# A new issue order for all engines of a post-LN attention and gated-MLP block, with the later weight loads behind the first sixteen spreads

## The chip, the cores and the metric
One NeuronCore of a Trainium2 chip runs the whole kernel in one launch. The metric is device time in microseconds (us). The kernel before takes 326.44 us, the median of 3 runs (326.33 to 326.91).

## The reference
x has shape (4, 512, 128), float32: four batches of 512 tokens. There are 16 heads of width 8.

```
qkv  = x @ qkv_w.T + qkv_b            # per head: q, k, v of width 8
attn = softmax(q @ k.T * 8**-0.5) @ v
x1   = layernorm(x + (attn @ fc_w.T + fc_b + x))
h    = silu(x1 @ w1.T * s1) * (x1 @ w2.T * s2)      # 128 -> 512
h    = gelu(h @ h1.T * t1)                          # 512 -> 512, exact gelu
h    = gelu(h @ h2.T * t2)                          # 512 -> 512
out  = layernorm(x1 + h @ w3.T * s3)                # 512 -> 128
```

## The kernel before
The work is cut into six units: batches 0 and 3 are two units of 256 tokens each, batches 1 and 2 one unit of 512 each. Every engine runs one list of named steps. The lists are text constants at the head of the file (`SP_ORDER`, `PE_ORDER`, `ACT_ORDER`, `DVE_ORDER`, `POOL_ORDER`, lines 8 to 52). `walk` reads them. A token `S:5` in the list of PE is step S with its result in PSUM bank 5, `H*3` is three further pieces of step H in the bank they already have, `zk*2` is two steps. The n-th time a name occurs, it is the n-th step of that kind (counted from 0, as S33 in the prediction). What a step computes and what it waits for is fixed by its name and number, whatever its place in the list. Engines take their list strictly in order, so the place decides what is queued behind a wait.

The steps that matter here:

- `x` transposes the 512 tokens of a batch (L443), `q` projects to q and to k (L532; two steps a batch), `v` to v (L537).
- q and k are split into bf16 parts on ACT, DVE and POOL: `q` and `da` (L728, L745), `r`, `mid`, `lo`, `db` (L857, L862, L866, L885), from batch 1 on also POOL's `da`, `mid`, `db`. The parts lie in `parts`. SP's DMAs spread them over the partitions of `stack` (L366, 128 KB each, two for each pair of heads). For batch 0 these are 16 single steps, `zq` and `zk`, eight for q and eight for k; a pair of heads needs its `zq` and its `zk`. The first `zq` waits for q's `lo` and copies, the first `zk` for k's. For batches 1 to 3 a step `spread` issues four DMAs for four heads, once the T steps of the batch before no longer read that part of `stack`.
- `S` (L479) is a tile of scores, 128 queries by 512 keys. DVE's step `s` (L852) takes its negated row maximum. When a group of heads is done, POOL's `m` splits the maxima, PE's `m` transposes them, ACT's `m` copies them and SP's `mrow` (L412) writes them into `stack` as one more row. There are 18 such groups, and the first needs 4 S tiles.
- `T` (L490) is the same scores transposed with the maximum already subtracted; its group waits for its `mrow`. ACT's `e` (L716) takes the exponential. `P` (L508) multiplies with v, `o`, `a`, `f` finish attention, and DVE's `l1` steps with POOL's `p1` make the layer norm x1. `X` transposes x1, `A` and `B` are the first two linear layers, `H` the two inner ones, `W` and `Y` the last (L468 for A, B, H and W), and `l2` with `p2` the second layer norm.
- `wt` transposes a 128 by 512 slab of weights (L443): number 0 and 1 are w1 and w2, 2 to 5 the four slabs of h1, 6 to 9 those of h2, 10 is w3. ACT copies it (L796), POOL splits it with `wc` and `wl` (L1017, L1020), and ACT's `wm` (L792) sums the magnitudes of the low part. After all eleven, DVE's `wx`, PE's `L` and DVE's `L` make a flag; PE reads it before the first `A`.
- SP loads with `lw` (w1, w2), `lh` (first h1, then h2, 1 MB each), `l3` (w3, into `y`), `more` (fc_b and the five scale vectors, six DMAs), `vb`, `xin` (the next batch's x), `xres` (the residual) and stores with `out`. `xres` n waits for x1 of the batch before it; `out` n waits for the n-th finished unit of the second layer norm. All of them, the spreads and the rows of maxima go through SP's one queue in the order of `SP_ORDER`.

Of the kernel before, what the change touches and what calls it, by code (L numbers as in the profile page):

```python
# [18 lines left out]
T:5 T:0 T:6 S:4 S:1 P T:2 S:3 T:5 S:4 T:0 S:6 H:1 H S:2 S:3 H*2 H:5 H*3 S:4 S:0 S:6 T:1 T:2 S:3 H:5 H m:4 H*2 H:0 H*3 S:4 S:1 S:6 S:2 P*2 S:3 S:5 S:0
T:4 T:1 S:6 o:2 q:7 a:3 q:2 f:5 S:4 T:3 T:0 T:1 H:6 H*3 H:5 H*2 T:7 S:3 T:2 T:0 T:1 S:6 S:4 H H:7 H T:3 T:2 S:6 S:0 H*2 H:1 H*3 X:4 S:3 S:2 S:6 S:5  # L20
S:7 m:0 P:1 A:3 B:4 A:2 A:6 B:0 A:5 P T:7 S:3 S:2 S:4 S:6 S:0 T:5 W:3 W*2 B:2 W S:7 S:4 B:5 Y:6 T:3 T:0 S:2 T:5 T:6 P T:3 S:7 S:0 T:4 T:5 T:2 P S:6
T:3 T:4 S:7 H:5 H T:0 S:2 S:6 T:3 H*2 H:4 H m:7 T:0 T:2 T:3 S:6 S:5 T:7 H*2 H:0 H*3 S:2 T:6 T:3 S:4 H:5 H*3 S:7 T:0 T:2 S:6 S:4 S:3 P*2 T:5 S:0 S:7
S:6 S:4 S:3 P*2 S:0 T:7 T:6 T:2 T:4 S:5 v:1 m:3 S:7 T:0 T:6 T:5 H:2 H*3 H:4 T:3 S:1 S:0 T:7 H*3 S:6 S:5 S:3 T:1 T:7 T:0 H:2 H*3 S:4 T:6 T:1 S:5 H:7
H*3 o:0 S:3 S:2 S:4 S:6 S:5 T:1 P:7 P*2 S:0 T:3 S:2 T:4 T:6 T:5 P S:1 T:3 T:0 T:4 P S:2 T:6 S:5 S:1 T:3 T:0 W:4 W m:2 W*2 T:6 S:5 T:3 T:2 T:1 S:0 Y:4
P S:5 S:6 S:3 T:0 T:4 T:2 P*2 S:1 T:0 T:5 S:4 x:6 o:2 T:3 T:7 S:1 S:0 T:5 T:4 a:2 T:3 S:6 S:1 f:0 m:2 S:7 T:6 T:5 T:1 T:4 T:0 T:3 P:2 S:6 S:5 T:1 v:7
T:4 T:0 T:6 T:3 X:1 q:4 S:7 S:0 q:6 A:3 A:5 A:1 A:4 B:7 B:6 B:3 B:5 S:7 S:1 T:6 P T:0 T:7 S:3 S:4 P T:6 S:1 S:5 S:3 T:0 T:4 P T:7 S:1 S:6 T:0 T:5 T:4
# [1038 lines left out]
```

## Time and profile before

| | |
|---|---|
| time, median of 3 | 326.44 us |
| the profiled execution's own time | 328.78 us |
| its span (first to last instruction) | 326.9 us |
| mean granted TensorE clock | 0.945 |
| PE / DVE / ACT / POOL busy | 291.2 / 244.2 / 246.1 / 169.4 us |

The span is 1.88 us shorter than the profiled execution's own time, which is 2.34 us over the median. Granted clock 1.00 is 2.4 GHz, 0.50 is 1.2 GHz. PE is busy for 89% of the span, but the ends of matmuls are modelled, and at the half clock a busy PE does half the work. The shares are means over three stages: the start (to about 31 us, when the first exponential runs), a long middle in which four batches of attention and MLP are mixed, and the tail (from about 290 us) in which only the last unit's MLP is left.

### The profile page before, as it was taken

To read this page: it belongs to the slowest core of one execution; us is meant where nothing else is said; L and a number is where in the kernel's file an instruction comes from. 1 tells how busy PE (TensorE), PEld (TensorE's weight loads), DVE (VectorE), ACT (ScalarE), POOL (GpSimd) and SP (SyncE) were. 2 spreads that over 40 slices of the span, in tenths; PEclk is the share of its full clock that TensorE was granted. 3 is DMA by queue.
4 is the path that set the end of the run, shared out by engine and by line. 5 is a ranking of instruction groups with operands and counts; after the bars stand their busy time and mean duration, and the time that the engine had idled before them with its cause. 6 is when DMAs were issued, how large, how long until landed. Compare 5 with 4: busy or idle time off the path is not lost.

```text
span 326.9 us, 6531 instructions
## 1 busy us (share of the span) xinstructions
PE 291.2 (89%) x2213; PEld 164.2 (50%) x2213; DVE 244.2 (75%) x531; ACT 246.1 (75%) x465; POOL 169.4 (52%) x287
## 2 busy tenths in 40 slices
...
PEclk9855899999999999999999999999799999997896
...
DMA packets 20276, 15.66 MB, mean 48 GB/s; under 512 B 2945, under 2 KB 19090, under 8 KB 20242
## 3 DMA queue, kind: packets, MB, share of 16 engines
...
q14 instruction: 14, 0.11, 0.1%
...
## 4 chain that ended last, share of the span: by engine, by line
PE 53%; DVE 15%; DMA 10%; ACT 9%; issue 5%; SPq 5%; POOL 1%; POOLq 0%; DVEq 0%; ACTq 0%
PE bank L468 23%; DVE negmax L852 9%; PE bank L479 8%; PE bank L508 8%; DMA stack<-parts 8%; PE bank L490 5%; ACT prob L716 4%; SPq L366 3%; PE bank L532 2%; DMA vb<-in_L_attn_qkv_b_dram 2%; PE bank L443 2%; DVE parts L866 1%; PE bank L461 1%; ACT L716 1%; PE bank L562 1%
## 5 line engine op out<-in xcount | busy, mean ns | idle before, releaser
L852 DVE TENSOR_REDUCE negmax<-bank 128x1 f32<-128x512 f32 x256 | 160.4, 680 | 35.7 <-PE bank L479 35.1
L716 ACT ACTIVATE prob<-bank 128x512 f32<-128x512 f32 x256 | 133.8, 616 | 11.2 <-PE bank L490 10.2
L468 PE MATMUL bank<-act,hT 128*128 128x256 f32 (+1 forms) x384 | 71.8, 332 | 0.6 <-POOL act L696 0.4
L479 PE MATMUL bank<-stack 64*128 64x512 bf16 x256 | 63.3, 402 | 8.8 <-DMA stack<-parts 7.9
L508 PE MATMUL bank<-prob,v_sb 128*32 128x256 f32 (+1 forms) x768 | 66.5, 456 | 0.3 <-ACT prob L716 0.2
L468 PEld LDWEIGHTS bank<-act,hT 128*128 128x128 f32 x384 | 55.8, 192 | 12.7 <-issue 4.7
L490 PE MATMUL bank<-stack 64*128 64x256 bf16 (+1 forms) x384 | 59.5, 311 | 2.7 <-DVE negmax L852 1.8
L693 POOL CAST act<-h_nat 128x256 fp32r<-128x256 f32 (+1 forms) x36 | 16.8, 497 | 45.7 <-ACT h_nat L782 45.7
L775 ACT ACTIVATE h_nat<-bank,hs_all 128x256 f32<-128x256 f32 (+1 forms) x48 | 25.5, 553 | 15.3 <-PE bank L468 15.1
L490 PEld LDWEIGHTS bank<-stack 64*128 64x128 bf16 x384 | 20.9, 94 | 32.0 <-issue 16.5
L479 PEld LDWEIGHTS bank<-stack 64*128 64x128 bf16 x256 | 16.1, 95 | 40.1 <-issue 20.9
L696 POOL TENSOR_TENSOR act<-h_nat,act 128x256 fp32r<-128x256 f32 (+1 forms) x36 | 34.2, 975 | 0.4
L508 PEld LDWEIGHTS bank<-prob,v_sb 128*32 128x32 f32 x768 | 21.2, 109 | 26.2 <-issue 15.8
L980 POOL TENSOR_TENSOR rstd<-rstd,mhalf 128x2 f32<-128x2 f32 (+1 forms) x12 | 10.8, 898 | 38.5 <-DVE rstd L833 38.4
L1008 POOL CAST mparts<-negmax 128x16 bf16<-128x16 f32 (+2 forms) x18 | 3.6, 199 | 43.1 <-DVE negmax L852 43.0
L1032 POOL TENSOR_TENSOR work<-work 128x256 f32<-128x256 f32 (+1 forms) x20 | 18.7, 955 | 11.1 <-ACT work L764 9.9
L468 PE MATMUL bank<-x1T,w12T 128*128 128x256 f32 (+1 forms) x96 | 21.4, 363 | 0.9 <-ACT prob L716 0.9
L925 DVE SCALAR_TENSOR_TENSOR work<-work,bank 128x256 f32<-128x256 f32 (+1 forms) x24 | 11.5, 504 | 12.9 <-ACT work L759 12.9
L468 PEld LDWEIGHTS bank<-x1T,w12T 128*128 128x128 f32 x96 | 16.9, 217 | 5.7 <-issue 2.1
L678 POOL TENSOR_TENSOR act<-work,act 128x256 fp32r<-128x256 f32 (+1 forms) x20 | 19.5, 1006 | 0.1
L759 ACT ACTIVATE work<-bank,hs 128x256 f32<-128x256 f32 (+1 forms) x24 | 12.1, 545 | 6.8 <-PE bank L468 6.6
L782 ACT ACTIVATE h_nat<-h_nat 128x1024 f32<-128x1024 f32 (+1 forms) x9 | 12.9, 1436 | 0.1
...
## 6 DMA issues: line engine op xcount, KB each, us to landing
...
h_nat<-in_L_ffn_h_w_dram SPq DMA_DIRECT2D x1, 1024.0 KB, 8.4
work<-in_L_ffn_h_w_dram SPq DMA_DIRECT2D x1, 1024.0 KB, 9.6
...
```

Source lines behind the costliest of these rows:

```text
L468: mm = nc.tensor.matmul(dst, w, v, start=first and n == 0, stop=last and n == len(pairs) - 1)
L479: nc.tensor.matmul(space("S", n)[:, :], stack[0][half_of(h), h // 2, qt * P:(qt + 1) * P], stack[1][half_of(h), h // 2, :], start=True, st ...
L490: last = nc.tensor.matmul(space("T", n)[:, c * w:(c + 1) * w], stack[1][half_of(h), h // 2, kt * P:(kt + 1) * P], stack[0][half_of(h), h / ...
L508: last = nc.tensor.matmul(space("P", pfirst)[at:at + VW, 0:w], v_sb[b % 2][:, kt, of:of + VW], prob[:, t % NP, c * w:(c + 1) * w], start=k ...
L678: do.tensor_tensor(a[1][:, k, cols(u)], gate[:, k, cols(u)], a[0][:, k, cols(u)].bitcast(F32), ALU.subtract).then_inc(lo0[e], 1)
L693: do.tensor_copy(a[0][:, k, cols(u)], raw[:, k, cols(u)]).then_inc(hi_g[e], 1)
L696: do.tensor_tensor(a[1][:, k, cols(u)], raw[:, k, cols(u)], a[0][:, k, cols(u)].bitcast(F32), ALU.subtract).then_inc(lo_g[e], 1)
L716: nc.scalar.activation(prob[:, n % NP, :], space("T", n)[:, :], ACT.Exp, scale=SCALE).then_inc(emptied("T", n), 1)
L775: nc.scalar.activation(raw[:, k, cols(u)], space(*h_first(u, layer, k))[:, 0:width(u)], ACT.Gelu if (u, layer) in DIRECT else ACT.Copy, sc ...
L782: nc.scalar.activation(r, r, ACT.Gelu).then_inc(gel_ok, 1)
L852: nc.vector.tensor_reduce(negmax[:, g % 2, col:col + 1], space("S", n)[:, :], AX.X, ALU.max, negate=True).then_inc(emptied("S", n), 1)
L1032: nc.gpsimd.tensor_tensor(gate[:, k, cols(u)], gate[:, k, cols(u)], up[:, n % 2, cols(u)], ALU.mult).then_inc(gate_ok, 1)
```

## The change
Only the five lists change. Each holds the same steps, equally often, and PE's bank numbers are new. SP's list whole, PE's up to the sixth line, and the first line of the others:

```diff
 SP_ORDER = """
 lw lh xin vb
-l3 more lh zq zk zq*2 zk zq zk*2 zq zk xres xin mrow zq zk zq*2 zk*2 mrow*4 xin spread mrow spread*2 mrow spread mrow*2 xres spread*2 mrow*2 spread*2
-out mrow*2 xres out spread*2 mrow spread*2 mrow*2 xres mrow*2 out*4"""
+zq zk*2 zq zk*2 zq*3 zk zq*3 mrow zk*3 mrow xin lh mrow l3 more mrow*2 xres spread mrow spread*3 mrow xin xres mrow*2 spread*2 mrow*2 spread*2 mrow
+xres out mrow spread*2 mrow spread*2 mrow*2 out xres mrow*2 out*4"""
 
 PE_ORDER = """
-x:0 wq:1 wf:2 q:3 q:4 v:5 wt:6 wt:7 wt:0 wt:1 wt:3 hs:4 x:6 wt:7 S:0 S:5 S:1 S:4 wt:2 S:6 S:0 S:5 S:1 S:4 S:6 m:3 q:0 S:7 S:3 S:5 wt:2 wt:1 S:4 m:6
-T:2 S:7 S:1 T:3 T:6 S:5 S:4 S:2 S:7 S:3 wt:6 wt:1 T:5 q:4 S:6 S:1 S:2 S:7 m:3 T:6 S:3 T:0 T:5 T:4 P:6 S:1 S:0 S:5 P S:2 T:7 T:3 T:4 S:1 S:0 P S:7 T:5
-T:3 S:2 S:4 T:1 P T:0 T:5 S:3 S:7 S:1 m:2 S:4 P*2 S:0 S:2 S:3 S:5 S:7 S:1 T:6 T:4 T:0 T:2 v:3 T:6 T:5 T:4 S:7 S:0 S:1 P:2 S:6 T:7 T:5 o:0 T:4 S:1 T:7
-m:3 S:5 T:6 T:4 S:3 P T:1 T:7 S:6 T:4 S:5 S:0 P S:3 S:1 T:7 T:6 T:4 S:5 P T:0 S:7 x:3 o:6 S:1 S:4 S:2 T:5 T:0 T:7 T:3 a:6 P:5 S:1 S:0 T:4 T:7 T:3 T:2
-f:6 L:1 P T:4 T:0 T:7 T:6 P S:3 S:2 S:1 m:4 X:0 P A:7 A:6 B:4 o:3 A:0 A:5 B:2 B:1 S:7 S:4 S:6 T:3 T:0 B:2 T:5 T:1 T:3 S:7 S:0 S:4 T:5 T:6 T:1 P:7 S:3
+x:2 wq:3 wf:4 q:5 q:6 v:0 wt:1 wt:7 wt:5 wt:6 wt:1 wt:2 x:4 S:7 S:0 S:3 S:6 S:7 S:4 S:1 
+S:0 S:5 m:6 S:7 S:3 S:4 S:1 S:6 S:0 S:2 q:5 q:7 S:4 S:1 m:3 T:6 T:3 S:0 S:2 T:6 T:3 m:6 S:1 S:4 S:3 P:0 P T:2 S:6 S:1 S:5 T:4 T:3
+T:2 P S:7 S:4 T:3 T:6 S:2 S:1 T:5 P S:7 T:3 S:6 S:4 T:5 T:2 wt:1 wt:3 S:5 S:7 S:2 v:6 m:4 S:5 hs:4 wt:7 wt:1 wt:2 T:3 S:5 S:7 T:1 S:4 S:3 P S:5 S:1
+S:6 T:2 T:7 P T:4 T:2 T:3 T:7 T:5 S:1 S:4 S:6 S:2 S:0 S:1 o:3 T:4 T:7 T:5 T:6 P:4 S:2 T:7 T:0 S:5 S:6 m:1 S:3 S:7 T:2 S:1 T:5 T:0 S:2 P*2 T:6 T:5 S:3
+S:0 S:7 T:1 P T:6 S:2 T:5 T:3 o:1 T:4 T:0 T:6 T:7 S:5 S:3 S:2 a:1 T:4 T:5 f:1 P:3 T:2 T:0 T:1 T:6 P L:7 m:4 X:5 P S:2 S:0 S:1 A:4 A:5 A:7 B:6 B:2 A:0
...
 ACT_ORDER = """
-x q*2 wt da*2 wt*3 wm*2 x wm*2 wt*2 m wt*3 wm m e*3 wt*2 q*2 m e*4 wm*2 e*8 m e o wm*3 e*10 m e*3 wm e*6 o e x e*4 a e*8 m o t*2 u t*2 u*2 e*8 u e*6
+x q*2 da*2 wt*2 x wt*3 wm wt m wm*3 m e*4 q*2 m e*10 wm m wt*4 e*2 wm wt wm e*4 o e*8 m e*4 wm*3 e*3 o e*4 a wm e*8 m e t*3 u*2 t o e*3 u e u e*6 x
...
 DVE_ORDER = """
-wq r mid r db mid lo db lo v hs wf s*22 r*2 s*15 lo s*11 v s*2 lo or s om s*8 or wx om s*5 l1*3 L l1*2 s Xh Xl s*2 t*2 or om t*2 s*23 or om s*3 l1 r*2
+wq r mid r lo mid db*2 lo wf v s*21 r*2 s*14 hs s v s*10 or s*2 om s*6 lo*2 s*4 or s om s*3 l1 wx l1*4 Xh Xl L s*3 t*4 s*2 or om s*22 or om s*3
...
 POOL_ORDER = """
 vz*2
-wc wl wc wl wc*2 wl*2 m wc wl m wc*2 wl*2 wc wl m xr wc*2 wl da mid*2 m wl wc wl da db m db m p1 u h0 u*2 h0 l0*2 h0 u l0 h0 l0 m gh*4 gl*4 da*2 mid
+wc*2 wl*2 wc*2 m wl wc*2 wl m*2 mid wl*2 m da wc wl db da mid db wc*2 wl*2 wc m wc wl*2 xr m p1 u*2 h0 l0 u*2 h0*2 l0*2 h0 l0 m gh*3 gl gh*3 gl*3 p1 mid
...
```

## Rows read from the trace of the kernel before

**Rows 1.** The page: busy time of PE, and its clock in 40 slices.
```profile
PE 291.2 (89%) x2213; PEld 164.2 (50%) x2213; DVE 244.2 (75%) x531; ACT 246.1 (75%) x465; POOL 169.4 (52%) x287
PEclk9855899999999999999999999999799999997896
```

**Rows 2.** The chain that ended last, 0 to 32 us: start, length, what.
```profile
12.43 1.02 DVE parts L866
...
13.50 7.54 DMA stack<-parts
...
21.08 1.11 PE bank L479 x4
```

**Rows 3.** Timeline of SP's queue: start, length, line, what, count.
```profile
4.80 0.51 SPq L418 DMA_DIRECT2D h_nat<-in_L_ffn_h_w_dram  x1
...
10.81 0.41 SPq L418 DMA_DIRECT2D work<-in_L_ffn_h_w_dram  x1
11.35 9.94 SPq L366 DMA_DIRECT2D stack<-parts  x10
...
26.07 1.32 SPq L412 DMA_DIRECT2D stack<-mT  x2
...
33.02 25.63 SPq L412 DMA_DIRECT2D stack<-mT  x8
```

**Rows 4.** The page: DMA issues, KB each, us to landing.
```profile
h_nat<-in_L_ffn_h_w_dram SPq DMA_DIRECT2D x1, 1024.0 KB, 8.4
work<-in_L_ffn_h_w_dram SPq DMA_DIRECT2D x1, 1024.0 KB, 9.6
```

**Rows 5.** The tile `stack`, 0 to 40 us: landing of its DMAs.
```profile
DMA to landing us min/median/max: 3.2/4.6/7.5
```

**Rows 6.** Timelines of DVE and POOL, 8 to 90 us, idle time before in brackets.
```profile
9.52 0.28 DVE L885 COPY parts<-parts 128x512 bf16<-128x512 bf16 x1
...
11.07 1.35 DVE L885 COPY parts<-parts 128x512 bf16<-128x512 bf16 x1
...
10.69 1.58 POOL L1020 TENSOR_TENSOR w12T<-x,w12T 128x512 fp32r<-128x512 f32 x1
...
21.73 6.07 DVE L852 TENSOR_REDUCE negmax<-bank 128x1 f32<-128x512 f32 x10 [3.23 <-PE bank L479]
...
70.01 0.60 DVE L842 TENSOR_SCALAR x<-res,mv,rstd 128x128 f32<-128x128 f32 x2 [0.82 <-POOL rstd L980]
```

**Rows 7.** Timeline of PE, 9 to 62 us.
```profile
13.32 1.50 PE L443 MATMUL bank<-ident,h_nat 128*128 128x128 f32 x12 [3.73 <-DMA h_nat<-in_L_ffn_h_w_dram]
...
16.38 1.11 PE L443 MATMUL bank<-ident,x_in 128*128 128x128 f32 x4
17.29 1.06 PE L443 MATMUL bank<-ident,h_nat 128*128 128x128 f32 x4
...
23.17 2.37 PE L479 MATMUL bank<-stack 64*128 64x512 bf16 x6
...
25.67 2.08 PE L532 MATMUL bank<-xT,qkvT 128*128 128x512 f32 x2
...
31.28 0.39 PE L490 MATMUL bank<-stack 64*128 64x256 bf16 x1
...
34.86 0.76 PE L443 MATMUL bank<-ident,y 128*128 128x128 f32 x4
...
45.11 1.06 PE L508 MATMUL bank<-prob,v_sb 128*32 128x256 f32 x8
```

**Rows 8.** Windows of 2 us: busy time of PE, PEld, DVE, ACT, POOL, granted clock, DMA share, GB/s.
```profile
34.00:36.00 2.00, 2.00 (x12) 1.62 (x12) 2.00 (x5) 0.90 (x2) 1.78 (x5) 0.71 0.36 75
```

**Rows 9.** Timelines of PE and SP, 60 to 200 us: waits for spreads, and a store.
```profile
71.65 0.60 PE L479 MATMUL bank<-stack 64*128 64x512 bf16 x3 [1.43 <-DMA stack<-parts]
...
127.28 0.60 PE L479 MATMUL bank<-stack 64*128 64x512 bf16 x3 [1.12 <-DMA stack<-parts]
...
196.16 0.82 PE L479 MATMUL bank<-stack 64*128 64x512 bf16 x5 [1.92 <-DMA stack<-parts]
...
188.95 0.39 SPq L435 DMA_DIRECT2D out_dram<-y  x1
```

More of the change, by code:

```diff
@@ L19 @@
[L19 to L26, printed above, removed]
@@ new lines @@
+S:0 S:7 T:1 P T:6 S:2 T:5 T:3 o:1 T:4 T:0 T:6 T:7 S:5 S:3 S:2 a:1 T:4 T:5 f:1 P:3 T:2 T:0 T:1 T:6 P L:7 m:4 X:5 P S:2 S:0 S:1 A:4 A:5 A:7 B:6 B:2 A:0
+P T:1 S:6 S:4 S:2 S:5 T:7 T:3 T:0 o:1 B:6 B:7 x:4 S:3 S:1 T:6 T:0 T:2 T:7 P:5 S:6 T:3 T:0 T:2 S:1 S:7 P S:3 T:6 T:0 T:1 T:4 S:7 H:2 H*2 S:6 S:3 T:0
+S:7 H H:1 H*3 S:4 S:6 S:2 S:3 H:7 H*3 m:1 H:0 H*3 S:4 S:6 S:1 S:2 S:7 S:3 P*2 T:0 T:4 S:6 S:1 S:2 o:5 q:7 a:3 q:5 f:6 T:0 T:3 T:1 T:2 H:4 H*3 H:6 H*3
+H:0 T:3 T:7 S:1 S:5 T:2 T:4 X:6 H*3 T:3 T:1 S:7 S:2 S:5 S:0 S:6 B:4 A:7 H:3 H A:2 A:1 H*2 m:4 A:5 B:0 S:7 S:4 P:2 S:3 S:1 T:6 S:0 S:7 S:4 P*2 T:3 S:1
@@ new lines @@
+S:0 B:7 B:4 T:6 T:5 T:3 S:1 S:7 W:4 W*2 T:0 S:6 W S:1 T:5 S:7 T:3 T:0 Y:6 m:4 S:1 S:5 T:6 T:3 T:4 P S:7 T:0 T:6 T:1 T:3 T:5 H:4 H*3 H:0 H*3 H:7 H S:6
+T:1 T:3 S:5 S:4 S:0 H*2 H:1 H*3 v:6 T:3 T:5 S:7 S:4 P S:1 S:0 S:6 S:7 P*2 T:4 S:1 S:0 S:6 T:3 T:5 T:7 P S:4 S:1 T:3 T:0 S:5 S:6 T:7 H:2 H*3 S:4 S:3
+S:1 T:0 T:5 T:7 H:2 H m:6 H T:0 T:4 H H:5 H T:6 T:3 T:7 S:0 S:1 S:2 H*2 H:4 H*3 o:0 S:6 S:3 S:1 S:7 S:2 T:5 P:4 P*2 S:0 S:6 T:3 T:1 S:7 T:2 P T:5 T:0
+S:3 S:6 T:1 T:7 P S:2 T:5 T:3 S:0 W:6 W*2 m:1 W S:7 T:2 T:5 T:0 T:3 T:1 Y:6 P T:2 S:5 S:6 S:0 P*2 S:3 T:7 T:1 T:2 T:5 S:6 o:0 x:4 T:3 S:7 a:1 T:2 S:0
@@ new lines @@
+S:4 T:6 f:7 T:1 T:5 m:0 v:3 T:4 T:2 T:7 S:6 T:0 S:1 P:5 T:4 S:6 T:2 T:7 q:1 X:0 q:4 S:2 T:3 P T:6 T:7 S:1 S:3 B:0 A:4 A:6 A:7 A:2 B:0 B:1 B:3 T:4 S:6
+S:7 P S:0 S:2 T:4 T:6 S:1 S:7 P T:3 T:0 S:4 S:2 T:6 T:1 P T:3 T:7 S:0 S:4 T:6 T:2 S:1 P m:3 T:0 S:7 S:4 S:6 S:2 T:1 P*2 S:3 S:0 T:7 T:1 T:4 T:6 T:2
+T:5 o:3 H:7 H*3 S:0 S:1 S:4 T:3 T:6 T:2 T:5 H:7 H*3 S:3 S:6 T:2 T:0 S:5 S:1 H:4 H*3 H:3 H*3 m:2 S:0 T:6 S:7 S:5 S:1 P:4 S:3 S:2 S:0 T:7 T:5 P*2 S:1
+S:3 S:2 S:0 T:6 T:1 S:7 T:3 T:5 P T:6 S:2 S:1 T:0 S:3 T:7 H:5 H T:6 T:2 T:0 S:1 T:7 T:3 H*2 H:6 H*2 T:1 T:2 T:0 T:7 T:5 m:3 H H:1 H*3 H:3 H*3 S:2 S:0
```

37 lines of the change are left out of this document (18 added, 19 removed).

## The prediction

> **What bounds the kernel now.** I read four views: the page for busy shares and the clock, the chain of waits for the start, the timelines of SP and PE behind it, and then only PE's idle gaps of more than half a microsecond in the rest. The page [rows 1] shows PE busy for 291.2 of 326.9 us, so 35.7 us are idle. The clock is at half speed in the third and fourth slice (16 to 33 us), partly in the second and fifth, and for a moment near 230 us and from 294 on. The middle is full: a step of one engine is hidden by another engine, and the order has little to give there. The start is not. Its chain [rows 2] goes from the low part of k on DVE through a DMA of 7.54 us to the first S at 21.08. The chain view puts the load of vb ahead of that DVE step; DVE was in fact busy with the copy of 11.07 [rows 6] until 12.42, so I take the copy as what held it. The reader should see in rows 3 to 5 why that DMA took 7.54 us when the median spread near it took 4.6: h2 (1 MB) was issued at 10.81, just ahead of the spreads, and landed after 9.6 us, at 20.4. The spreads landed right behind it. PE stood idle meanwhile.
>
> **Start: the first S.** The change moves h2, w3, and the six small loads (SP steps lh, l3, more) behind all sixteen batch-0 spreads and two rows of maxima. Two things must then be ready for the first S.
> The spreads: k's low part ended at 12.43 + 1.02 = 13.45 [rows 2]. ACT now does both da before the first wt, so POOL's first wc starts later than DVE's copies. The copy that took 1.35 us beside POOL's 1.58 us step took 0.28 at 9.52 [rows 6]: 1.07 less, thus 12.4. A spread then takes 3.2 to 7.5 us, median 4.6 [rows 5]: 12.4 + 4.6 = 17.0.
> PE itself: six wt and x now stand ahead of the first S, as before. h1 landed at 4.80 + 8.4 = 13.2 [rows 3, 4]. From 13.32: three wt in 1.50, the fourth 1.06, x 1.11 at half clock [rows 7] = 17.0 also.
> So the first S comes at 17.0 instead of 21.08: -4.1. Bounds: 0 where the spreads still take 7.5 us (12.4 + 7.5 = 19.9, and k's part no sooner: 21.0), and -5.5 where they take 3.2 and h1 lands sooner.
>
> The 0.28 and 1.35 us rows are weighed against a rule. The Trainium skill (SBUF — State Buffer, Who interferes with whom) says that a DVE copy in its two-port modes and a GpSimd instruction lock each other out of one shared port pair, the second waiting until the first ends. The copy indeed ended 0.15 us after POOL's step did. By that rule the gain of 1.07 hangs on POOL still being idle at about 11.2 us; if wc and wl come just before the copies, the sum's first term is -3.0 instead of -4.1, unless PE's own 17.0 decides, in which case nothing changes.
>
> **From the first S to the first T.** Before: 21.08 to 31.28 = 10.2 us, and PE did 14 S, three wt, one q and two m in it. After: 18 S, two q and two m, no wt. At half clock an S costs 2.37 / 6 = 0.395 and a q 1.04 [rows 7]: 7.1 + 2.1 + 0.5 = 9.7 us. DVE takes 0.607 for an s [rows 6] and trails within the eight banks, 18 - 4 of them make 8.5. PE decides: the first T at 17.0 + 9.7 = 26.7. The row of maxima must be there: mrow 0 is now queued on SP behind thirteen spreads (ten before). From 13.5 the last nine of the first ten took to 21.29, 0.87 each [rows 3]; twelve from 12.4 end at 22.8; the two DMAs of mrow take 1.32 [rows 3], to 24.1; they landed in under 31.28 - 27.39 = 3.9 us. So T could be held until 28.0 at worst. I take 26.7, which is -4.6 in all, bound -3.3.
> At that T four more S are done (4 x 0.607 = 2.4 us of DVE), but three wt are not (3 x 0.76 = 2.3 us of PE [rows 7]). I count these against each other: 0, bounds -2.4 and +2.3.
>
> **h2 and the moved small loads.** h2 now stands behind mrow 1 and xin. With m 1 right ahead of the first T, mrow 1 goes at 27.0 to 28.3, xin and lh follow within about 1.2 us, and 9.6 us [rows 4] later, at 39.1, h2 is there. PE wants it after 33 S, 14 T and four P; the fourth P ended at 46.2 before [rows 7], so at 41.6 now. No wait: 0, bound +1. Cover is 2.5 us; if it goes, all of PE's list stands behind wt 6. l3 and more (seven DMAs on SP's queue) run before mrow 3, which waited in the stretch from 33.02 on anyway [rows 3].
>
> **Batch border.** The first S of batch 1 waited 1.43 us for its spread [rows 9]. This chain (last T that reads the old stack, four DMAs, landing) is the same, but X of unit 0 and the flag L now stand in front of these S, and x1 comes from DVE and POOL, where DVE itself waited 0.82 [rows 6]. The one wait hides in the other. I take 0, bounds -1.4 and +1.4.
>
> **Two later waits that the order removes.** From m 8 to the first S of batch 2 PE had 10 S, 9 T, 10 H and 2 P, and waited 1.12 us for the spread, which is issued behind mrow 8. Now it has 13 S, 13 T, 16 H, 4 P and a v there. And the first spread of batch 3 stood behind out 1 (188.95) on SP, that is behind the second layer norm of unit 1, for a wait of 1.92 [rows 9]; now out 1 is behind mrow 15 and the spread waits only for mrow 12 and the T steps of batch 2. Together 3.0 us of PE's idle time. DVE and ACT are nearly full around both, so another engine is late next; I take half, -1.5, bounds 0 and -3.0.
>
> **The rest.** Same steps, other neighbours. PE's tail from X of unit 5 on holds the same steps in nearly the same places. Everything after the start hangs on dependences alone, so an earlier start is carried through. For the new waits that a new order of five lists brings I put +0.9, since the nearest rows show single waits of 1.1 to 1.9 us [rows 9]; bounds -2 and +4.
>
> Sum: -4.6 - 1.5 + 0.9 = -5.2 us. The profiled execution took 328.78 (span 326.9 and 1.88 around it), so 323.6; it was 2.34 above the median of the runs, and against these 326.44 - 5.2 = **321.2 us**. The likeliest case's own range is 319.2 to 323.2.
>
> **Rivals.**
> *The first T is held* (0.14). The spreads land at SP's pace and mrow 0 behind thirteen of them is late, or POOL holds the copies. For it: T at 28.0, and first S at 17 to 19.9. Against: h2 is gone from in front of them. First T gains 2 to 3, the later waits return as others: -2.4, 324.0 us.
> *The middle gives more* (0.11). Both later waits count in full and the +0.9 isn't there: -4.6 - 3.0 - 0.5 = about -8, 318.4 us.
> *The clock stays low* (0.09), the one that ends slower. It fell after PE had stood idle from 9.6 to 13.3 us, which the change doesn't touch, and was back at 34 to 36 us [rows 8], just after four slabs of weight transposes (16 matmuls from 28.6 to 35.6) mixed with S and T. The change puts these, and the slab before them, behind S33, leaving single S with pauses for DVE. Where PE bounds, each us at 1.2 GHz instead of 2.4 costs half a us. In the forecast the clock comes back about 4 us after the first T, at 31, as it did before (31.28 to 35.4). This rival decides the sign once it stays low 10 us longer (to 41 us); at 14 us more it costs 7: +2, 328.4 us. Against it: once T and P run, PE is as busy as it was at 35.
> The Trainium skill (TensorE: Matmul & The Clock Gate, HAM oscillation) tells that the half rate is the default and sustained work releases it. By that rule the sparse S stretch alone would not release it and the forecast's 31 us hangs on T and P following at once; the trace agrees in so far as the clock did not return in the S stretch of 21 to 26 us.
> *The new middle gives back the start* (0.11): waits like those of rows 9 appear in three to five new places, e.g. X of unit 0 or wt 6: 326.4 us, half of it within 0.2%, half slower.
>
> **Chances.** Forecast 0.55, the others 0.14, 0.11, 0.09 and 0.11. Faster by over 0.2% (0.65 us, about what this measurement can tell from no change): 0.55 + 0.14 + 0.11 = 0.80. Within: 0.06. Slower: 0.09 + 0.05 = 0.14. The range 317.8 to 326.0 leaves out the clock rival, half of the last one and the far end of the good side, 0.18 in all.
>
> **What would show it.** SP's timeline: sixteen spreads from about 11 us without h2 in front. First S at 16.5 to 17.5; a wait of PE on the spreads of under 1 us before it. DVE's second copy (L885) at 0.28. First T (L490) at 26 to 28, granted clock back at 1.00 by 32. No wait of PE at wt 6 near 41. No wait near 123 and 191 us where rows 9 had theirs. A first S after 19.5, a wait of over 2 us on h2, or half clock past 36 us would prove steps wrong; so would new waits of more than 4 us in sum between 60 and 290 us.

## The result, and the profile after

The changed kernel takes 315.87 us, the median of 4 runs (313.29 to 317.33); the kernel before took 326.68 in the same comparison. The ratio is 0.966, with a 95% interval of 0.958 to 0.974. A repeat of the changed kernel (e17 below) gave 316.54 us and 0.969 [0.964, 0.975]. The forecast was 321.2, in a range of 317.8 to 326.0: the sign was right, and the time lies below the range.

The profiled execution of the changed kernel took 316.08 us, its span is 314.2 and its mean granted clock 0.969. The one of before was 2.3 us above its median, so the spans differ by 12.7 us and the medians by 10.8. The page of the changed kernel, its line of busy times and the clock in 40 slices, answers to [rows 1]:

```profile
PE 286.5 (91%) x2213; PEld 162.6 (52%) x2213; DVE 237.5 (76%) x531; ACT 244.8 (78%) x465; POOL 169.0 (54%) x287
PEclk9968999999999999999999999999999999996996
```

The clock is low from 18.6 to 25.4 us, from 284.8 to 291.6 and from 308.7 to the end; the low place that the kernel before has near 230 us is gone. The work is the same, and PE and DVE are each busy for less time: PE because fewer of its products run at half clock, DVE for a reason shown below. (Two lines of the change as printed above are not exactly those of the changed kernel: in the first line of DVE's list it has `s*21 r s*2 r s*14`, and in the first long line of POOL's `gh*3 gl gh gl*3 p1 mid`.)

Where the time went is read best from windows cut at the same PE steps in both. The cuts are the first S, the first T, and f 0 to f 5 (the product that ends each unit's attention); the columns are length, busy time of PE, PEld, DVE, ACT, POOL, granted clock, DMA share, GB/s. The kernel before:

```profile
0.00:21.08 21.08, 12.23 (x82) 9.93 (x83) 9.79 (x21) 11.53 (x22) 12.34 (x25) 0.85 0.79 231
21.08:31.28 10.20, 10.11 (x31) 3.83 (x31) 8.05 (x14) 1.98 (x5) 6.47 (x14) 0.50 0.56 109
31.28:66.85 35.57, 33.62 (x314) 15.98 (x313) 34.10 (x65) 29.51 (x67) 17.29 (x31) 0.95 0.14 30
94.63:158.17 63.54, 59.87 (x436) 29.70 (x435) 56.14 (x113) 58.03 (x110) 33.86 (x72) 1.00 0.22 38
158.17:222.43 64.26, 59.56 (x370) 27.95 (x370) 49.49 (x93) 53.49 (x93) 34.71 (x49) 1.00 0.27 45
222.43:263.66 41.23, 39.08 (x322) 22.80 (x322) 32.82 (x73) 33.00 (x59) 26.18 (x33) 0.96 0.03 9
294.61:326.94 32.33, 21.10 (x140) 19.20 (x138) 20.39 (x71) 10.61 (x21) 8.39 (x12) 0.82 0.06 18
```

The changed kernel, cut at the same steps:

```profile
0.00:15.80 15.80, 11.14 (x81) 9.26 (x82) 6.15 (x18) 6.48 (x10) 8.21 (x21) 1.00 0.72 188
15.80:26.32 10.52, 8.04 (x24) 2.48 (x25) 9.66 (x16) 5.21 (x14) 6.26 (x14) 0.68 0.70 128
26.32:61.07 34.75, 32.74 (x302) 15.79 (x301) 33.30 (x65) 29.64 (x66) 20.89 (x34) 1.00 0.26 70
88.90:148.96 60.06, 59.29 (x433) 29.82 (x431) 54.21 (x111) 56.68 (x108) 33.48 (x68) 1.00 0.22 37
148.96:212.32 63.36, 60.32 (x376) 27.99 (x375) 48.93 (x95) 54.01 (x94) 36.99 (x53) 1.00 0.27 46
212.32:251.30 38.98, 38.15 (x323) 22.34 (x323) 32.54 (x74) 32.97 (x60) 26.30 (x34) 1.00 0.04 13
281.95:314.24 32.29, 20.57 (x140) 18.79 (x138) 20.21 (x74) 10.71 (x21) 7.24 (x12) 0.81 0.07 18
```

Length before minus length after gives 5.28 up to the first S, then -0.32 and 0.82: 5.8 us at f 0. Of the two stretches left out, f 0 to f 1 gives nothing and f 4 to f 5 gives 0.3. Between them come 3.48, 0.90 and 2.25: 6.6 us from three stretches of the middle. The forecast had 0.6 for everything behind the first T. In the first of the three PE's idle time (length minus PE's busy time) went from 3.67 to 0.77 us. The last stretch is the same to 0.04 us.

One pair of traces overstates the start. Ten of the profiles here, that of the kernel before among them, have the old order up to f 0; they have their first T at 28.7 to 31.3 us (mean 30.3) and f 0 at 64.3 to 67.9 (mean 65.6). Eight have the changed kernel's lists up to f 0, with nothing added; theirs are 25.4 to 27.7 (mean 26.4) and 60.8 to 64.9 (mean 62.2). So on average the start gives 3.9 us at the first T and 3.4 at f 0, and the profile of the kernel before was one of the late ones.

The start in detail: DVE's, SP's and PE's timelines of the changed kernel, which answer to [rows 3, 6, 7]. Columns: start, length, what, and in brackets the idle time before it and what ended it.

```profile
10.71 0.49 DVE L885 COPY parts<-parts 128x512 bf16<-128x512 bf16 x2
11.12 0.68 DVE L866 TENSOR_TENSOR parts<-qk_r,parts 128x512 bf16<-128x512 f32 x1
...
11.10 11.58 SPq L366 DMA_DIRECT2D stack<-parts  x13
22.73 1.85 SPq L412 DMA_DIRECT2D stack<-mT  x2
...
28.67 0.50 SPq L418 DMA_DIRECT2D work<-in_L_ffn_h_w_dram  x1
...
13.23 1.94 PE L443 MATMUL bank<-ident,h_nat 128*128 128x128 f32 x16 [3.37 <-DMA h_nat<-in_L_ffn_h_w_dram]
15.00 0.60 PE L443 MATMUL bank<-ident,x_in 128*128 128x128 f32 x4
15.80 0.60 PE L479 MATMUL bank<-stack 64*128 64x512 bf16 x3 [0.20 <-DMA stack<-parts]
...
19.95 0.60 PE L479 MATMUL bank<-stack 64*128 64x512 bf16 x1 [1.41 <-DMA stack<-parts]
...
26.32 0.70 PE L490 MATMUL bank<-stack 64*128 64x256 bf16 x3
...
37.03 1.09 PE L443 MATMUL bank<-ident,work 128*128 128x128 f32 x8
```

The spreads run from 11.10 with nothing large ahead of them, both DVE copies take the short time, and h2 is issued at 28.67; landing after 7.3 us, it is there at 36.0, 1 us before PE's `wt` at 37.03 asks for it. The landing of the spreads, the same row as [rows 5], is now

```profile
DMA to landing us min/median/max: 3.1/3.8/5.2
```

### The profile page after: what moved, and what is told of

Same layout as the page of the kernel before. It is cut to its first block, busy times and chain, and to the rows that moved or that the text cites. A ratio compares the mean times of both kernels' runs of the same rounds, so it can differ in the third digit from the quotient of the medians.

```text
span 314.2 us, 6531 instructions
## 1 busy us (share of the span) xinstructions
PE 286.5 (91%) x2213; PEld 162.6 (52%) x2213; DVE 237.5 (76%) x531; ACT 244.8 (78%) x465; POOL 169.0 (54%) x287
## 4 chain that ended last, share of the span: by engine, by line
PE 60%; ACT 9%; DVE 9%; DMA 6%; POOL 6%; issue 5%; SPq 4%; POOLq 0%; DVEq 0%; ACTq 0%
PE bank L468 24%; PE bank L508 11%; PE bank L490 8%; PE bank L479 8%; DVE negmax L852 5%; ACT prob L716 4%; DMA stack<-parts 2%; PE bank L532 2%; SPq L366 2%; POOL act L678 2%; DMA vb<-in_L_attn_qkv_b_dram 2%; DMA stack<-mT 2%; PE bank L461 2%; PE bank L562 1%; ACT L716 1%
## 5 line engine op out<-in xcount | busy, mean ns | idle before, releaser
L468 PE MATMUL bank<-act,hT 128*128 128x256 f32 (+1 forms) x384 | 70.4, 329 | 0.6 <-POOL act L696 0.3
L479 PE MATMUL bank<-stack 64*128 64x512 bf16 x256 | 58.9, 388 | 4.4 <-DMA stack<-parts 3.0
L490 PEld LDWEIGHTS bank<-stack 64*128 64x128 bf16 x384 | 21.1, 94 | 31.4 <-issue 14.6
L479 PEld LDWEIGHTS bank<-stack 64*128 64x128 bf16 x256 | 16.7, 94 | 35.7 <-issue 22.0
L980 POOL TENSOR_TENSOR rstd<-rstd,mhalf 128x2 f32<-128x2 f32 (+1 forms) x12 | 9.7, 806 | 28.7 <-DVE rstd L833 28.7
L468 PE MATMUL bank<-x1T,w12T 128*128 128x256 f32 (+1 forms) x96 | 19.9, 350 | 0.4 <-issue 0.4
L678 POOL TENSOR_TENSOR act<-work,act 128x256 fp32r<-128x256 f32 (+1 forms) x20 | 18.8, 960 | 0.2
L468 PEld LDWEIGHTS bank<-x1T,w12T 128*128 128x128 f32 x96 | 16.1, 211 | 4.3 <-issue 1.8
L892 DVE RECIPROCAL rden<-bank 128x16 f32<-128x16 f32 (+1 forms) x12 | 3.4, 286 | 12.7 <-PE bank L549 12.7
```

What stands on the lines that cost most here:

```text
L468: mm = nc.tensor.matmul(dst, w, v, start=first and n == 0, stop=last and n == len(pairs) - 1)
L479: nc.tensor.matmul(space("S", n)[:, :], stack[0][half_of(h), h // 2, qt * P:(qt + 1) * P], stack[1][half_of(h), h // 2, :], start=True, st ...
L490: last = nc.tensor.matmul(space("T", n)[:, c * w:(c + 1) * w], stack[1][half_of(h), h // 2, kt * P:(kt + 1) * P], stack[0][half_of(h), h / ...
L678: do.tensor_tensor(a[1][:, k, cols(u)], gate[:, k, cols(u)], a[0][:, k, cols(u)].bitcast(F32), ALU.subtract).then_inc(lo0[e], 1)
```

## Why the middle got shorter: what the two traces show

I compared the long waits of PE that the old middle has and the new one lacks. Besides the two later waits on spreads of [rows 9] (127.28 and 196.16), there are three on DVE, and at each of them DVE is slow beside a tensor operation of POOL. The kernel before, DVE, POOL and PE at three places (110 to 119, 178 to 190 and 225 to 230 us):

```profile
114.08 1.93 DVE L833 TENSOR_SCALAR rstd<-mv 128x2 f32<-128x2 f32 x1
...
113.17 2.81 POOL L678 TENSOR_TENSOR act<-work,act 128x256 fp32r<-128x256 f32 x4
...
116.65 0.39 PE L490 MATMUL bank<-stack 64*128 64x512 bf16 x1 [1.07 <-DVE negmax L852]
...
180.24 2.74 DVE L866 TENSOR_TENSOR parts<-qk_r,parts 128x512 bf16<-128x512 f32 x2
...
180.72 4.64 POOL L678 TENSOR_TENSOR act<-work,act 128x512 fp32r<-128x512 f32 x3
...
183.72 0.63 PE L549 MATMUL bank<-ident,oT 128*128 128x128 f32 x4 [1.49 <-DVE negmax L852]
...
188.22 0.62 POOL L991 COPY parts<-parts 128x512 bf16<-128x512 bf16 x1
...
226.98 2.06 DVE L842 TENSOR_SCALAR x<-res,mv,rstd 128x128 f32<-128x128 f32 x4
...
226.91 1.27 POOL L696 TENSOR_TENSOR act<-h_nat,act 128x512 fp32r<-128x512 f32 x1
...
229.09 0.66 PE L461 MATMUL bank<-ident,x 128*128 128x128 f32 x4 [1.61 <-DVE x L842]
```

L833 touches two numbers a partition. Its twelve instances, here in the view of that line (min/median/max in ns), show one that took eleven times the median, until 116.01, when POOL's row of four ended at 115.98:

```profile
L833 DVE TENSOR_SCALAR rstd<-mv x12: 146/169/1931, 69.0 to 322.0; 128x2 f32<-128x2 f32 x8, 128x4 f32<-128x4 f32 x4
```

In the changed kernel the same view has 567 at most:

```profile
L833 DVE TENSOR_SCALAR rstd<-mv x12: 152/170/567, 63.0 to 308.8; 128x2 f32<-128x2 f32 x8, 128x4 f32<-128x4 f32 x4
```

The four x steps of the fourth unit take little over half of their 2.06 us there, and PE's last long wait for a spread, which answers to the 1.92 of [rows 9], is 1.20. DVE's and PE's timelines of the changed kernel:

```profile
216.86 1.12 DVE L842 TENSOR_SCALAR x<-res,mv,rstd 128x128 f32<-128x128 f32 x4
...
185.26 0.47 PE L479 MATMUL bank<-stack 64*128 64x512 bf16 x2 [1.20 <-DMA stack<-parts]
```

The Trainium skill (SBUF — State Buffer, Who interferes with whom) says that a tensor_scalar in a two-port mode, or a DVE instruction with two SBUF inputs, and a GpSimd instruction that reads SBUF exclude each other on one pair of ports, the one waiting until the other's instruction ends. The rows agree with the exclusion, but not with its length: L833, started at 114.08 in a row of four POOL operations of 0.70 us, ended only with the last of them. That L833 runs in such a mode is not shown by any row. The rows also show where it hurt: where PE stood behind that DVE step. The theory tested below (A) is that the middle's gain comes from a handful of places at which one step stood in the way of PE, by such a lock or by order. The rival (B) is that the whole new order gives it, each wait removed alone coming back at the next place.

## The experiments

All ratios are to the kernel before on the same chip, with a 95% interval. A time alone is the median of the runs. Several chips were used, so times of two experiments are compared by their ratios where their chips differ. In the expectations TensorE, VectorE and GpSimd are PE, DVE and POOL, a mask row is a row of maxima, and a seam is a joint of two orders. Where an experiment's lists take fewer lines of text, its line numbers are lower by one to three. The first group splits the change by time: the five lists are joined at one step, with the new order on one side.

**e1: the new order up to f 0, the old one behind it.**

```diff
-each list: the old steps up to f 0
+each list: the changed kernel's steps up to f 0
 each list: the old steps from there on
```

> All five lists take the new order up to the first f step (61 us of the changed kernel's trace) and keep the old order of every later step. Theory A (the traces add up: the start is worth 5.3 to 5.8 us at that f, and the rest of the 12.7 us of span comes from the new order of the middle): 5 to 6.5 us less than before, about 320.7. Rival B (the start alone moves everything, because a middle that is reached earlier also loses its waits): 10 to 12 us less, about 315.5.

328.30 us, ratio 1.007 [1.003, 1.011]: slower than before, which neither theory had.

**e2: the other way round, old up to f 0, new behind it.**

> The reverse: old order up to the first f step (67 us), new order of every later step. Theory A: the part of the gain that lies behind the first f, 6.9 us of span, so about 319.7, and first S still at 21 us. Rival B (the middle gains only because of the start): within 1.5 us of before.

320.75 us, ratio 0.982 [0.976, 0.989]. So the new rest alone is worth 5.8 us (0.0176 x 327; by the interval 3.6 to 7.8), more than the 5.2 that the forecast had for all. e1 reaches f 0 4.8 us earlier than before and loses it at the joint, PE's timeline of e1:

```profile
65.88 1.94 PE L505 MATMUL bank<-prob,v_sb 128*32 128x256 f32 x16 [2.73 <-ACT prob L713]
```

A window of e1 from 64.8 to 71.7 us has a granted clock of 0.51. ACT came to the joint late; that the new start leaves it less far ahead than the old rest needs is my reading and was not tested. e1 therefore says nothing on the value of the start, and e3 does.

**e3: the changed kernel with the later loads ahead of the spreads, on SP alone.**

```diff
-zq zk*2 zq ... mrow xin lh mrow l3 more mrow*2
+l3 more lh zq zk*2 zq ... mrow xin mrow mrow*2
```

> The changed kernel with one edit in SP's list: w3, the small loads and h2 are issued again before the first spread, as in the kernel before. Theory A (the place of the loads alone makes the first S come at 15.8 instead of 21.1): first S at 20.5 to 21.5, and the time 4.5 to 5.5 us over the changed kernel, about 321. Rival C (the new order of PE, ACT and DVE makes the earlier start, the loads do little): less than 2 us over the changed kernel.

320.85 us, ratio 0.984 [0.978, 0.990], against 0.966 and 0.969 of the changed kernel. The first S falls back to 20.34, PE's timeline of e3:

```profile
20.34 1.11 PE L479 MATMUL bank<-stack 64*128 64x512 bf16 x4 [4.31 <-DMA stack<-parts]
```

The place of h2 and the small loads is thus worth about 5 us (0.015 x 327 = 4.9 against e17), near the forecast's -4.6. Start and rest together, 5 and 5.8, make the 10.8 measured, closer than two numbers of this width need to: e3 and e17 ran on different chips, and each ratio can be off by 0.6%. The first spread of e3 is issued at 11.24, the first of the changed kernel at 11.10. So the issues of the moved loads cost nothing there, and the landing of the spreads is what got longer, with the same row as [rows 5] at 3.1/4.8/8.3 in e3 against 3.1/3.8/5.2. Which of the eight loads does it, h2 or the small ones, was not separated.

**e11, e5, e6: three further joints.** In e11 the new order reaches to the first A steps of unit 0; in e5 it stands only between f 1 and f 2, in e6 only between f 2 and f 4.

```diff
-each list: the old steps of that stretch
+each list: the changed kernel's steps of that stretch
```

> The new order of all lists up to the first A steps (68 us of the changed kernel's trace, so past the first S of batch 1), then the old order. The cut at the first f lost its gain in a gap of PE of 2.73 us and half clock from 64.8 to 71.7 us, both right behind the seam. Theory A (that loss was the seam's): 4.5 to 6.5 us less than before, first S of batch 1 at 65 to 67 us. Rival S (the old middle gives the start back by itself): less than 2 us under before.

> Old order but for the stretch from f 1 to f 2 (96 to 158 us), which has the new order of all engines. In the traces of the two kernels this stretch is 3.48 us shorter with the new order. Theory A (stages add up): 2.5 to 3.7 us less than before. Rival R (it gains only with its own past): within 1 us of before.

> Old order but for the stretch from f 2 to f 4 (158 to 264 us), which has the new order of all engines. In the traces of the two kernels this stretch is 3.15 us shorter with the new order. Theory A (stages add up): 2.5 to 3.5 us less than before. Rival R (the stretch gains only with what comes before it in the new order): within 1 us of before.

327.84 us, 1.001 [0.998, 1.005]; 332.35 us, 1.014 [1.006, 1.023]; 327.52 us, 1.000 [0.996, 1.004]. None gives what its stretch promised. e11 has X of unit 0 3.8 us earlier than before and f 1 0.6 us later. In e5 the stretch from f 1 to f 2 is 0.9 us shorter than before and not 3.5, PE waiting 2.58 us for DVE at 96.28 right behind the joint; from f 2 to X of unit 2 it then takes 2.45 us longer than before. That profile is of a run of 327.66, 4.7 us below e5's median, so most of what e5 loses is not in it. In e6 X of unit 2 comes 5 us later behind f 2 than before, with PE waiting 0.88 for DVE and 1.42 for ACT and a stretch at half clock; this profile is of a run of 330.15, 2.6 us above the median. A stretch of an order is not worth the same before another neighbour. For this reason the rest of the experiments moves single steps.

**e4: the old kernel with only `out` 1 moved.** The forecast put the wait of 1.92 us of [rows 9] down to it.

```diff
-out mrow*2 xres out spread*2 ... mrow*2 xres mrow*2 out*4
+out mrow*2 xres spread*2 ... mrow*2 out xres mrow*2 out*4
```

> The kernel before with one edit in SP's list: the second store of y (out 1) is issued behind mrow 15 instead of in front of the first spread of batch 3, as the change does. Theory A (the spread stood behind that store, and PE waited 1.92 us for it): the wait at 196 us is gone, 1 to 2 us less than before. Rival D (DVE and ACT are nearly full there, the wait only moves): within 0.5 us of before.

326.66 us, 1.002 [0.997, 1.006], no change. The wait became 1.32. The other 1.3 us were not the store: in the rows of before above, POOL's copy (L991) ends at 188.84, because it stands behind POOL's residual, and the spread cannot go before it.

**e10, e9: one move each.** e10 puts DVE's `l2` 3, whose rstd step took 1.93 us, behind s 116. e9 puts POOL's `gl` 23 ahead of the p1 of the fourth unit, so that it no longer runs beside DVE's x steps.

```diff
 DVE_ORDER (e10)
-s*5 l2 s*3 l2*2 s l2 s*5 lo*2 s*15
+s*5 l2 s*3 l2*2 s*5 l2 s lo*2 s*15
 POOL_ORDER (e9)
-gh*4 gl*3 p1 gl m
+gh*4 gl*4 p1 m
```

> The kernel before with one DVE step (L833 of unit 0's second layer norm) four s steps later, past POOL's four low parts. Theory P: it takes 0.16 instead of 1.93 us and PE's wait of 1.07 us at 116.6 goes: 1 to 1.7 us less than before at the second S of batch 2. Rival Q: the 1.8 us reappear as waits for PE within the next 20 us, same time.

> The kernel before with one swap in POOL's list: gl 23 ahead of p1 3, the reciprocal root for the first layer norm of unit 3. POOL was idle for 1.50 us ahead of p1, and gl beside the DVE step L842 made it 2.06 us for four. Theory P: these four come to 1.3 us, X of unit 3 about 0.9 us sooner, PE's gap of 1.61 us gets under 0.8 and the clock, which fell at 229.7 for 3.4 us, may stay up: 0.9 to 2.6 us less than before. Rival Q: within 0.5 us.

326.70 us and 325.98 us, both 0.997 (e10 [0.993, 1.001], e9 [0.994, 1.000]). Neither is clear of no change, and both are less than expected. The profiles show each at its place: in e10, no L833 takes more than 0.35 us and m 8 comes 1.5 us earlier, counted from f 1, but PE's next wait for a spread grows from 1.12 to 1.71, so part of it comes back there; in e9 the four x steps take 1.11 us in place of 2.06:

```profile
227.80 1.11 DVE L841 TENSOR_SCALAR x<-res,mv,rstd 128x128 f32<-128x128 f32 x4
```

**e8: both moves, `out` 1, and `l2` 9 behind s 187.**

```diff
 DVE_ORDER, beside e10, e9 and e4
-s*12 lo*2 s*5 l2 or s*2 om
+s*12 lo*2 s*5 or s*2 l2 om
```

> The kernel before with four single steps moved and nothing else: DVE's third layer-norm step of unit 0 (L833, 1.93 us instead of 0.16 beside POOL's low parts) four s steps later; DVE's last step of unit 1's second layer norm (L842, 1.6 us for two) behind the next two s; POOL's p1 of unit 3 behind its last low part, so that L842 (2.06 us for four) has POOL idle; and out 1 behind mrow 15. Theory P (the old middle loses its time where DVE steps with two SBUF operands or a two-port mode stand beside POOL's, and the new order happens to avoid these): 3 to 5 us less than before, the three stretched steps at 0.16, 0.3 and 0.35 us each, no half clock near 230 us. Rival Q (the gain is spread over the whole order of the middle): within 1 us of before.

324.08 us, 0.992 [0.989, 0.996]: 2.5 us, where 3 to 5 had been expected. There is no half clock near 230 us. Waits of about 1 us are left on PE, among them 1.47 for DVE at 180.86 and 1.33 for the spread at 192.71.

**e14: e8 with one of DVE's low parts two s steps earlier (`lo` 4) and two of them three s steps later (`lo` 6, 7), POOL's copy ahead of the residual, and two spreads each ahead of a row of maxima on SP. e18: the same without these two moves on SP.** e14's expectation lists `lo` 5 too; in the list it keeps its place among the s steps.

```diff
 DVE_ORDER
-l2*2 s*5 l2 s lo*2 s*15
+l2*2 s*4 lo s l2 s lo s*15
-s*12 lo*2 s*5 or s*2 l2
+s*15 lo*2 s*2 or s*2 l2
 POOL_ORDER
-db xr db m
+db*2 xr m
 SP_ORDER (e14 only)
-spread mrow*2 xres spread*2 mrow*2 spread*2
+spread mrow spread mrow xres spread mrow spread mrow spread
```

> The kernel before with the four single moves of e8 and seven more: on VectorE lo 4 and lo 5 stand right behind s 115 instead of s 117 and lo 6 and lo 7 behind s 183, on GpSimd db 5 stands ahead of xr 2, and on SP spread 4 stands ahead of mrow 8 and spread 6 ahead of mrow 10. Theory A, that the gain of the new middle is that of a handful of places where TensorE waits in the old one: the waits at S128 (0.99 left in e8), S160 and S192 go, 5 to 6 us below the kernel before, about 321. Rival B, that the gain needs the whole order: what one place gives back is waited for at the next, no more than e8 (ratio 0.992, about 324). Rival C: the earlier spreads hold up the mrow transfers behind them, and VectorE's moved steps hold the scores, slower than e8.

> e14 without its two moves on SP: mask rows and spreads stand in the order of the kernel before (e14's profile shows spread 4's issues ahead of mask row 8 from 116.8, the mask row issued at 120.24 and TensorE waiting 3.56 us for it). Theory A: the moves on VectorE and GpSimd keep what they gave behind f 2 (S192 2.3 us earlier after f 2 than in e8) and the SP move's loss goes: about 321.5, ratio 0.983 to 0.986, so near the 0.982 of the new rest. Rival B: without the SP moves the earlier low parts and copies give nothing, and the time is e8's, ratio 0.992.

e14: 323.16 us, 0.989 [0.985, 0.994]. e18: 321.71 us, 0.982 [0.976, 0.987]. In e14 SP's four issues take from 116.79 to 120.19, and the row of maxima that PE needs next is issued behind them (SP's and PE's timelines of e14):

```profile
116.79 3.40 SPq L364 DMA_DIRECT2D stack<-parts  x4
120.24 0.67 SPq L410 DMA_DIRECT2D stack<-mT  x1
...
123.60 0.42 PE L488 MATMUL bank<-stack 64*128 64x512 bf16 x1 [3.56 <-DMA stack<-mT]
```

e18 keeps SP's order. Counted from f 2, its spread of batch 3 goes 2.3 us earlier than in e8 (28.4 us behind f 2, against 30.7), and PE's two waits on spreads are 0.77 and 0.39 us. PE's, DVE's and SP's timelines of e18:

```profile
123.72 0.60 PE L478 MATMUL bank<-stack 64*128 64x512 bf16 x3 [0.77 <-DMA stack<-parts]
189.45 0.82 PE L478 MATMUL bank<-stack 64*128 64x512 bf16 x5 [0.39 <-DMA stack<-parts]
...
179.52 2.72 DVE L865 TENSOR_TENSOR parts<-qk_r,parts 128x512 bf16<-128x512 f32 x2
...
182.78 7.11 SPq L365 DMA_DIRECT2D stack<-parts  x8
```

So eight single steps in the old order (`out` 1, `l2` 3 and 9, `lo` 4, 6 and 7, `db` 5, `gl` 23) give the 0.982 that the whole new rest gave in e2. Theory B falls: the whole order is not needed. Theory A holds as far as this: a handful of steps is enough for a gain of that size. That the new order's own gain lies at the same places is not shown, and by stretches it does not look the same: from f 1 to f 4 e18's three stretches are 1.8, 2.8 and 2.2 us shorter than before, the changed kernel's 3.5, 0.9 and 2.3. One more thing is to be seen in these rows: the two low parts still take 2.72 us beside POOL. They do no harm, since the maxima that PE waits for are now ahead of them. For this place it was the position that mattered, not the stretching. (The moves of e18 beyond e8 were not tried one by one.)

**e15: the changed kernel with `gl` 23 put back behind p1.** The reverse of e9.

```diff
-gl*2 gh gl*2 p1 m
+gl*2 gh gl p1 gl m
```

> The changed kernel with one step of GpSimd put back as in the kernel before: the first p1 of the fourth unit stands ahead of gl 23 again, so that GpSimd's products run beside VectorE's four x steps. Theory A (VectorE's steps stretch beside GpSimd's products): the four x steps at 216.9 take about 2 us each instead of 1.1, the first X behind them starts 0.9 us later, and where that wait brings TensorE's half clock with it, 1.7 us more: 0.9 to 2.6 us above the changed kernel. Rival B: in the changed kernel this place has slack, and the time stays within 0.5 us of the changed kernel's.

319.90 us, 0.981 [0.975, 0.986]: 3.4 us above e17 on the same chip, more than expected. The four x steps stretch as they should, to 2.05 us for all four. But PE's own order is another than in the kernel before and asks for that low part earlier. DVE's and PE's timelines of e15:

```profile
216.70 2.05 DVE L841 TENSOR_SCALAR x<-res,mv,rstd 128x128 f32<-128x128 f32 x4
...
217.95 0.73 PE L467 MATMUL bank<-act,w3T 128*128 128x512 f32 x2 [2.19 <-POOL act L695]
```

POOL's p1 waits for DVE's rstd, and `gl` 23 waits behind it. So the size of e15 is mostly the order of POOL, and only the 2.05 speaks for the ports.

**e12, e13: zero products in PE's idle time.** After f 5 PE waits 3.11 us for DVE's x steps, in the changed kernel as in the one before, and then runs at half clock. e12 puts 13 `K` steps there, each four small products with a zero operand, whose results nothing reads; e13 has 14 more ahead of the wait for h1.

```diff
+K:6 (13 times, e12 and e13)
 X:6 H:0 A:2 B:3 ...
 wt:1 wt:7
+K:2 (14 times, e13 only)
 wt:5 wt:6 wt:1
```

> The changed kernel with 13 steps of four zero products each put between the last f and the last X on PE (their results are read by nobody). PE waits 3.11 us there for x1 and its clock is at half for 6.8 us just behind. Theory T (the idle wait is what drops the clock): clock 1.00 through the last unit's MLP, 2 to 3.4 us less than the changed kernel. Rival U (the clock falls anyway, or the last MLP is bound by ACT and DVE): within 0.7 us.

> As the one before, and 14 more such steps where PE waits for h1 (9.9 to 13.2 us). Theory T: half clock from 18.6 to 25.4 us goes or comes later, first T 0.5 to 2 us sooner, total 0 to 2 us less than with the tail's alone. Rival V (the start is bound by spreads and DVE): same as with the tail's alone.

318.17 us, 0.973 [0.966, 0.980], and 318.45 us, 0.976 [0.969, 0.982], neither better than the changed kernel. I had the steps too short: they took 0.46 us each, so that X comes 2.7 us late, and behind it the tail is 1.7 us shorter. The first S of e12 comes at 17.46, 1.7 us later than in the changed kernel's profile, although nothing is changed there; the part on the prediction comes back to it. In e13 the first S comes 0.8 us later still than in e12, and the higher clock there (0.984 over the span) leaves the time where e12 has it.

**e16: 6 such steps; e17: the changed kernel again; e19: e16 with one `l0` behind POOL's copies.**

```diff
+K:6 K:6 K:6 K:6 K:6 K:6
 X:6 H:0 A:2 B:3 ...
 POOL_ORDER (e19)
-l0*4 mid db mid db m
+l0*3 mid db mid db l0 m
```

> The changed kernel with 6 steps of products with a zero operand put ahead of the last X, where TensorE waits 3.11 us for VectorE; by e12, whose 13 steps took 0.46 us each, 6 take about 2.8 us and fit the wait. They add zero and change no result. Theory A (the half clock behind that wait comes from the idle time alone): no half clock at 284.8 to 291.6, the last stretch 1.7 us shorter as in e12, and nothing lost ahead of it: 1.5 us below the changed kernel. Rival B: the clock falls all the same or the last stretch is held by other engines once TensorE is faster: within 0.5 us of the changed kernel.

> The changed kernel once more, beside the others on the same chip. Both theories: the ratio to the kernel before as first measured, 0.966, about 315.9 us; if it differs by more than 0.5%, the differences between this and the other experiments are read with that width.

> The changed kernel with the 6 zero steps of e16 and one step of GpSimd moved: the last l0 of the third unit (1.28 us at 173.7) stands behind the copies that the first spread of batch 3 waits for, not ahead of them, so that this spread is issued 0.6 us earlier (VectorE is free at 175.0, its first low part started at 175.58). Theory A: the wait of 1.20 us at S192 shrinks to 0.6 us or less, the moved l0 is there in time, 0.6 us below e16, about 314.4. Rival B: TensorE's products at 176.9 or 179.9 need that l0, which now ends at about 178.5, and wait for it: 0 to 1.5 us above e16.

e16: 314.97 us, 0.965 [0.960, 0.970]; e17: 316.54 us, 0.969 [0.964, 0.975]. The window of 284.8 to 291.6 us, of e16 and then of the changed kernel:

```profile
284.80:291.60 6.80, 5.48 (x45) 4.83 (x45) 4.41 (x12) 3.09 (x7) 5.82 (x10) 1.00 0.01 2
```

```profile
284.80:291.60 6.80, 5.58 (x24) 5.06 (x25) 4.52 (x13) 2.08 (x5) 5.16 (x10) 0.50 0.00 0
```

At full clock PE gets through 36 products where it did 24 (9 of the 45 are zero products). From f 5 to the end e16 takes 30.44 us and this execution of the changed kernel 32.29. The one profiled as e17 has the same wait of 3.11 us, but its clock fell only at 287.8 and was back at 291.3, and its last stretch takes 31.4. The same window of e17:

```profile
284.80:291.60 6.80, 5.38 (x29) 5.07 (x30) 5.09 (x15) 2.16 (x6) 5.16 (x9) 0.75 0.00 0
```

So the filling is worth 1.0 to 1.8 us in the traces. The medians differ by 1.6 us in the expected direction, but the two intervals overlap, so e16 is the likely best version and not shown to be better by the time alone.

e19: 320.79 us, 0.979 [0.974, 0.985], some 4.8 us worse than e16 by the ratios, and worse than its rival B had it. The spread was not the point: PE needs that low part first. PE's timeline of e19:

```profile
180.91 1.06 PE L468 MATMUL bank<-act,hT 128*128 128x512 f32 x2 [2.75 <-POOL act L678]
```

## Why the prediction was wrong

*The first S.* The mechanism was right, the size short by 1.2 us: forecast 17.0, measured 15.80. The copies took 0.25 each, and k's low part 0.68 where it had taken 1.02 [rows 2]; so it ended at 11.80 instead of 12.4, and its first spread landed in under 4 us. PE was ready at 15.6, since in this execution its four slabs and x ran at full clock where I had priced them at half. That is not a property of the change. Of the eight profiles with this start, the four in which the clock held have their first S at 15.5 to 15.8, the four in which it fell during the slabs at 16.3 to 17.5. The length of the wait for h1 doesn't decide it: it held behind 3.15 to 3.37 us and fell behind 2.38, 2.52, 3.06 and 3.93. PE's timeline of e12, one of those that fell:

```profile
13.03 3.65 PE L443 MATMUL bank<-ident,h_nat 128*128 128x128 f32 x16 [3.06 <-DMA h_nat<-in_L_ffn_h_w_dram]
```

*From there to the first T.* Forecast 26.7, measured 26.32, and the closeness is luck, since several errors nearly cancel. The first S was 1.2 us early. The stretch behind it, forecast at 9.7 us, took 10.52. In it the later spreads of the first sixteen landed one by one (PE waited 1.41 at 19.95), which the sum had not; and the sum's price of a q was half of the real one. The row of 2.08 in [rows 7] is two products and one q step, so two q at half clock are 4.2 us and not 2.1; they took 3.41, part of it at full clock. Against that several S ran at full clock. The clock came back at 25.4 us, not at 31, and 0.9 us before the first T: so its return didn't hang on T and P following, as the prediction had reasoned, and it was the S and q steps from 19.95 on, without a pause, that went ahead of it. The Trainium skill has the rule that the prediction names there, that activity releases the half rate, in an earlier section (TensorE: Matmul & The Clock Gate, What's actually happening). The return at 25.4 agrees with it; that the clock of the kernel before came back only at 35.2, though PE had hardly paused since 21.08, it does not explain. Counted at S 64 the lead in this pair of traces is 5.6 us where I had 4.6; on average over the profiles it is 3.9 at the first T. That the place of the loads makes the early start is settled by e3.

*h2.* No wait, as forecast, with 1 us of cover, not 2.5: PE came to `wt` 6 at 37.0, not at 41.6.

*The failed step* is the one under "The rest", that the order of the middle would cost 0.9 us, with the sentence ahead of it that the middle "is full" and "the order has little to give there". The forecast for the middle was -1.5 + 0.9 = -0.6 us; from f 0 on the chip gained 5.8 us (e2). I read PE's idle gaps of over half a microsecond in the middle, and the three on DVE (1.07, 1.49, 1.61 us) were among them. I took only those on spreads as removable, because a queue was visible in front of them; for the others I saw a busy engine and didn't ask why that step was slow, or whether it had to stand ahead of what PE waited for. A step of 128x2 that takes 1.93 us was there to be seen. What the runs showed in its place: eight steps put elsewhere in the old order are worth as much as the new rest, 0.982 (e18); they stand at these waits and at those on spreads.

*The two later waits.* I counted half of 3.0 us on the ground that another engine would be late next. The first went whole. The second fell from 1.92 to 1.20. Its cause was wrong, too: e4 shows `out` 1 to be 0.6 us of it; most of the rest went in e18, where POOL's copy stands ahead of the residual and 0.39 us of the wait is left.

*The rivals.* "The middle gives more" (0.11) was the right one in direction, and its 318.4 us still 2.5 short, since it was built from the two known waits alone. "The clock stays low" and "the new middle gives back the start" fell. In e1, e5, e6 and e11 something like the latter happened, where two orders that were not made for each other meet; in the change itself nothing was given back.

*What stays open.* The 0.82 us between the first T and f 0 was not tested by itself. Why e1's ACT is late at the joint was read from the trace only. Why the clock falls during the slabs in some executions and not in others is open.
